# Written-out cross loops, later attention products, and plain expert writes with a read-back, in a three-layer kernel on one core

## The chip, the cores and the metric

The kernel runs on one NeuronCore of a Trainium2 chip. The core has a matmul engine (TensorE, PE in the rows; PEld is its weight load), VectorE (DVE), ScalarE (ACT), GpSimd (POOL), SyncE (SP, which here only starts transfers) and 16 DMA engines. Each engine runs its own stream of instructions; semaphores tie the streams together. The metric is the device time of one execution in microseconds (us). The kernel before takes 898.19 us, the median of three runs between 898.18 and 898.23.

## The reference

x has 32 batches of 32 tokens of width 512 (1024 rows), the context 32 batches of 257 rows. All is fp32.

```
x = x + cross_attention(layernorm(x), ctx)   # 16 heads of 32; q and k are rotated by position;
                                             # softmax over 257 keys; output projection and bias
x = x + self_attention(layernorm(x))         # 16 heads, causal, 32 tokens
n = layernorm(x)
logits = n @ gate_w.T + gate_b               # 8 experts
keep the 2 best experts per row; gate = softmax over these 2
x = x + sum over the 2 of gate[e] * (n @ expert_w[e] + expert_b[e])
```

## The kernel before, in words

**Products.** An fp32 product is made of three products of parts: each operand is split into a high part (rounded by ACT) and a low part (the rest, by DVE or POOL), and `mm3` adds hi x hi, hi x lo and lo x hi over four chunks of 128, 12 matmuls in one PSUM bank. Names that end in `hi` or `lo`, and `wparts`, are such parts.

**Cross stage.** A tile is 128 rows of x, 4 batches; there are 8 tiles, so 32 batches b = 4t + j. `body(t)` writes out the four batches of a tile. Body 0 and body 7 stand in the program as straight code; bodies 1 to 6 are one body in a hardware loop (`Fori`) on each of the five engines, so every engine jumps back five times. For one batch PE does, in this order: the scores of b (64 matmuls on 32x32 pieces of the array, into four banks); K of b+1 (four `mm3`, 48 matmuls); the transposes of the probabilities of b; V of b+1, first half (12 matmuls, lines 723 to 725); one extra product that differs with j (output projection of the tile before, transposes of the normalised rows, q, transposes of q); attention `attend(b)` (64 small matmuls, line 759); `diagonals_spread(b)` (line 767), which spreads the last key's probability and the inverse sum; and V of b+1, second half. On the other engines: ACT evacuates K (`kb`), makes the exponentials (`pr`) and copies the transposed probabilities (`pt`); DVE masks the scores and takes their maximum (`scored`, `nmax`), inverts the sums (`rinv`), makes `kcos`, evacuates V, and in `o_sum` and `o_lo` adds the last key's part, normalises the attention output (`olast`, `osum`, `onorm`) and makes its low part (`otlo`); POOL makes `ksin` and the diagonals (`pdiag`). The scores of b+1 wait for `kcos` and `ksin`. Order on every engine is the order of the code.

**Self attention** is a pipeline over the 8 tiles; the change leaves it as it is. After it DVE computes the routing: a table that gives for each of 23 slots of 128 rows the expert, the row numbers to gather, and the gate of each row. Every row of x appears in two slots, once per chosen expert. Slots that are not full have spare rows.

**Expert stage.** POOL gathers the 128 normalised rows of slot i from the scratch tensor `ffn_xn_scratch` by an indirect DMA (line 1074) into one of four buffers, three slots ahead. PE transposes the rows of slot i+1 (line 1538, 4 matmuls), then multiplies slot i with its expert's matrix (lines 150 to 152, 12 matmuls). ACT and DVE split the transposed rows (lines 1215 and 1518); ACT multiplies the product by the gate into one of two buffers, called `qt` and `kt` (line 1223). POOL then adds it to the rows of `out_dram` by an indirect DMA with an accumulate (line 1087). Since a row may be in two slots, each add first waits for the one before (`s_add`). The small copies and "ticks" on POOL (lines 1064, 1071, 1081) go between the waits and fetch one column of row numbers. Before the first add, SP has stored all of x with the expert biases in it to `out_dram` (lines 1005, 1006); POOL waits for these nine stores.

## Time and profile before

| what | value |
|---|---|
| runs | 898.18, 898.19, 898.23 us |
| the profiled execution: time, span | 897.09 us, 895.3 us |
| mean granted clock of TensorE | 0.944 |
| busy: PE, PE weight load, DVE, ACT, POOL | 792.0, 649.6, 445.3, 346.4, 307.1 us |
| cross stage, self attention and routing, slots, rest | 0 to 585.4, to 766, to 883.2, to 895.3 us |
| DMA queue of SP: data moved | 43.92 MB |
| DMA queue of POOL: data moved | 12.06 MB |

The span is the time from the first to the last instruction of the profiled execution; its time is 1.8 us more. A granted clock of 1.0 is TensorE's full 2.4 GHz, 0.5 is 1.2 GHz. Durations of matmuls overlap, so the distance between two starts tells more than a duration. In a wait, "issue" as releaser means that the engine waited for nothing that the profile shows.

### The profile page before, as it was taken

How to read it: one execution, taken by the hardware profiler on the slowest of the kernel's cores; microseconds unless marked ns; L12 is line 12 of the kernel's file. 1: busy time of each engine (PE TensorE's matmuls, PEld its weight loads, DVE VectorE, ACT ScalarE, POOL GpSimd, SP SyncE). 2: the span in 40 equal slices, each digit the busy share in tenths (PEclk: the TensorE clock that was granted, in tenths of full speed). 3: DMA queues.
4: the chain of work that ended last, by engine and by line, in shares of the span. 5: the costliest groups of instructions: out<-in, count | busy, mean ns of one | idle time of the engine just before them, and what ended most of it. 6: DMA issues, size and time to landing. Idle time of an engine off the chain costs nothing. (4 is left out here: it accounts for less than half of the span.)

```text
span 895.3 us, 22458 instructions
## 1 busy us (share of the span) xinstructions
PE 792.0 (88%) x8896; PEld 649.6 (73%) x8897; DVE 445.3 (50%) x1102; ACT 346.4 (39%) x807; POOL 307.1 (34%) x357
## 2 busy tenths in 40 slices
PE   5999999999999899999989999969999717777764
PEld 5888888888888788788878888847777515555553
DVE  5645645444454564554444555566766589111110
ACT  5434433433433444335334444434454640222221
POOL 1322422332232223223322332232223084477763
PEclk9999999999999999999999999999999755889987
DMA  9430100100010001001000102172000101655553
GB/s 338 169 119 26 49 25 26 44 31 25 27 49 25 27 25 49 27 26 48 27 26 26 30 21 96 48 300 90 22 14 12 37 12 31 165 100 95 103 104 50
DMA packets 18072, 57.33 MB, mean 64 GB/s; under 512 B 2552, under 2 KB 2936, under 8 KB 16064
## 3 DMA queue, kind: packets, MB, share of 16 engines
q1 hardware_dynamic: 12832, 43.92, 13.6%
q0 software_dynamic: 5152, 12.06, 7.6%
q8 instruction: 76, 1.25, 0.6%
q14 instruction: 12, 0.10, 0.0%
HBM read 45.49 MB, written 10.49 MB: 63 GB/s over the span
## 5 line engine op out<-in xcount | busy, mean ns | idle before, releaser
L150 PE MATMUL bank<-chi,wparts 128*128 128x258 f32 x512 | 152.5, 298 | 7.4 <-DVE wparts L606 7.4
L151 PE MATMUL bank<-clo,wparts 128*128 128x258 f32 x512 | 148.1, 289 | 0.0
L152 PE MATMUL bank<-chi,wparts 128*128 128x258 f32 x512 | 148.0, 289 | 0.0
L318 POOL TENSOR_TENSOR pdiag<-pr,const 128x128 f32<-128x128 f32 x32 | 13.0, 408 | 357.4 <-ACT pr L379 357.4
L150 PEld LDWEIGHTS bank<-chi,wparts 128*128 128x128 f32 x512 | 100.4, 196 | 20.8 <-issue 13.4
L312 POOL TENSOR_TENSOR ksin<-kb,const 128x1032 f32<-128x1032 f32 x32 | 98.5, 3078 | 37.0 <-ACT kb L371 37.0
L723 PE MATMUL bank<-wparts,chi 128*128 128x512 f32 x256 | 110.0, 430 | 1.3 <-DVE wparts L589 1.3
L724 PE MATMUL bank<-wparts,chi 128*128 128x512 f32 x256 | 101.1, 395 | 0.0
L151 PEld LDWEIGHTS bank<-clo,wparts 128*128 128x128 f32 x512 | 100.9, 197 | 0.0
L725 PE MATMUL bank<-wparts,clo 128*128 128x512 f32 x256 | 100.8, 394 | 0.0
L152 PEld LDWEIGHTS bank<-chi,wparts 128*128 128x128 f32 x512 | 100.7, 197 | 0.0
L379 ACT ACTIVATE pr<-scored,nmax 128x257 f32<-128x257 f32 x128 | 63.8, 502 | 54.4 <-DVE nmax L549 54.4
L371 ACT ACTIVATE kb<-bank,bias_cols 128x258 f32<-128x258 f32 x128 | 60.5, 473 | 51.1 <-PE bank L152 50.8
L539 DVE TENSOR_TENSOR v<-bank,bias_cross 128x512 f32<-128x512 f32 x64 | 44.1, 689 | 72.5 <-PE bank L725 72.5
L533 DVE TENSOR_TENSOR kcos<-kb,const 128x1032 f32<-128x1032 f32 x32 | 50.4, 1576 | 34.2 <-ACT kb L371 34.2
L392 ACT ACTIVATE othi<-onorm 128x128 fp32r<-128x128 f32 x32 | 9.9, 311 | 136.7 <-DVE onorm L568 136.7
L723 PEld LDWEIGHTS bank<-wparts,chi 128*128 128x128 f32 x256 | 48.6, 190 | 11.2 <-DVE wparts L589 1.7
L725 PEld LDWEIGHTS bank<-wparts,clo 128*128 128x128 f32 x256 | 48.2, 188 | 11.5
L724 PEld LDWEIGHTS bank<-wparts,chi 128*128 128x128 f32 x256 | 48.4, 189 | 9.0
L364 ACT ACTIVATE chi<-craw 128x1032 fp32r<-128x1032 f32 x32 | 34.0, 1064 | 45.9 <-PE bank L725 41.7
L150 PE MATMUL quad<-wparts,othi 128*128 128x512 f32 (+1 forms) x108 | 46.0, 426 | 2.7 <-issue 2.6
L490 DVE TENSOR_TENSOR clo<-craw,chi 128x1032 fp32r<-128x1032 f32 x32 | 45.7, 1430 | 5.2 <-ACT chi L364 5.2
(233 smaller groups left out, 1712.9 us busy)
## 6 DMA issues: line engine op xcount, KB each, us to landing
craw<-ctx_t_dram SPq DMA_DIRECT2D x32, 516.0 KB, 3.3
expert_lo<-weights_dram SPq DMA_DIRECT2D x8, 1024.0 KB, 13.2
wraw<-weights_dram SPq DMA_DIRECT2D x7, 1024.0 KB, 6.1
out_dram<-x SPq DMA_DIRECT2D x9, 256.0 KB, 5.0
x<-x_dram SPq DMA_DIRECT2D x8, 256.0 KB, 7.4
ffn_xn_scratch<-xn SPq DMA_DIRECT2D x8, 256.0 KB, 2.0
wraw<-weights_dram SPq DMA_DIRECT2D x4, 256.0 KB, 5.4
craw<-biases_dram SPq DMA_DIRECT2D x2, 512.0 KB, 4.6
```

The costliest lines, as they stand in the source:

```text
L150: pe.matmul(psum, ahi(c), bhi(c), start=(c == 0), stop=False)
L151: pe.matmul(psum, ahi(c), blo(c), start=False, stop=False)
L152: last = pe.matmul(psum, alo(c), bhi(c), start=False, stop=(c == chunks - 1))
L312: pool.tensor_tensor(ksin[:], kb[:], sink, ALU.mult).then_inc(s_ksin, 1)
L371: act.activation(kb[:, m, :], proj[m % 3][:, 0:LKP], ACT.Identity, bias=bias_cols[:, m:m + 1]).then_inc(s_kev, 1)
L379: act.activation(pr[:, g, 0:LK], sm[g][:], ACT.Exp, bias=nmax[:, g:g + 1], scale=-1.0, accum_out=rsum[:, g:g + 1]).then_inc(s_exp, 1)
L490: dve.tensor_tensor(clo[j % 2][:], craw[j % 2][:], chi[j % 2][:].bitcast(F32), ALU.subtract).then_inc(s_clo, 1)
L533: dve.tensor_tensor(kcos[:], kb[:], cosk, ALU.mult).then_inc(s_kcos, 1)
L539: dve.tensor_tensor(v[j % 2][:, c, :], proj[(4 + c) % 3][:], bias[:, R_BV, :], ALU.add).then_inc(s_vev, 1)
L723: pe.matmul(psum, hi, whi[WV][:, c, :], start=(c == 0), stop=False)
L724: pe.matmul(psum, hi, wlo[WV][:, c, :], start=False, stop=False)
L725: last = pe.matmul(psum, lo, whi[WV][:, c, :], start=False, stop=(c == KC - 1))
```

## The change

It has four parts.

1. The cross stage's hardware loop over tiles 1 to 6 becomes written-out code on all five engines.
2. In the cross stage PE does V's second half right after the first half and the extra product, then `diagonals_spread(b)`, then `attend(b)`, then the scores of b+1. `o_sum(b)`, ACT's `o_hi(b)` and `o_lo(b)` move into batch b+1, behind its masked scores. A signal on PE before the scores and the tick writes on DVE between them go. At the start DVE makes WV's low parts before `kcos`.
3. In the expert stage POOL writes each slot's output with a plain indirect DMA to a scratch tensor `ffn_out_scratch`, in which a row's first and second choice have rows of their own, and spare rows have others. A slot's buffer is one of four (`qt`, `kt`, `q_self`, `k_self`). No write waits for another. The copies and ticks on POOL go, and the slot loops on POOL and ACT are written out; those on PE and DVE stay. The normalised rows are stored one row further down, and row 0 is a filler.
4. The nine early stores of x go. At the end SP waits for all writes, loads both choices of each tile back (16 loads of 256 KB into the space of `expert_lo`), DVE adds them to x (16 additions), and SP stores x (8 stores).

```diff
@@ cross stage (the same on SP, POOL, ACT, DVE, PE)
-                with pe.Fori(1, TILES - 1) as t:
+                for t in range(1, TILES - 1):
                     body(t)
@@ cross stage, PE
-                    pe.sem_inc(s_go, 1)
...
-                        attend(b, j)
-                        diagonals_spread(b)
                         if more:
                             v_product(b + 1, j + 1, 1)
+                        diagonals_spread(b)
+                        attend(b, j)
@@ cross stage, ACT
                         exp(b, 3)
+                        if not (j == 0 and at_start(t)):
+                            o_hi(b - 1, t if j > 0 else t - 1, (j + BT - 1) % BT)
...
-                        o_hi(b, t, j)
@@ cross stage, DVE
-                    dve.memset(tick[:, g:g + 1], 0.0)
...
-                    dve.wait_ge(s_spread, b + 1)
+                    dve.wait_ge(s_av, b + 1)
...
+                w_lo_chunks(WV)
                 k_cos(0)
-                w_lo_chunks(WV)
...
                             masked(b, j, g)
+                        if not (first and j == 0):
+                            o_sum(b - 1)
                         inverse_sums(b)
+                        if not (first and j == 0):
+                            o_lo(b - 1, (j + BT - 1) % BT)
...
-                        o_sum(b)
-                        o_lo(b, j)
@@ expert stage, SP
-                for t in range(TILES):
-                    sp.wait_ge(s_xbias, t + 1)
-                    sp.dma_start(out[t * P:(t + 1) * P, :], x[:, t, :]).then_inc(s_init, 16)
-                sp.dma_start(out[B * S:B * S + P, :], x[:, 0, :]).then_inc(s_init, 16)
+                sp.wait_ge(s_y, SLOTS)
+                for r in range(AHEAD):
+                    sp.wait_ge(s_scatter[r], 16 * len(range(r, SLOTS, AHEAD)))
+                for t in range(TILES):
+                    for k in range(2):
+                        row = 1 + k * B * S + t * P
+                        sp.dma_start(halves[:, 2 * t + k, :], y_d[row:row + P, :]).then_inc(s_half[t // 2], 16)
+                for t in range(TILES):
+                    sp.wait_ge(s_choices, 2 * t + 2)
+                    sp.dma_start(out[t * P:(t + 1) * P, :], x[:, t, :]).then_inc(s_stored, 16)
@@ expert stage, POOL
-                    pool.wait_ge(s_yev, i + 1)
-                    tick(2)
-                    pool.tensor_copy(add_at[r][:], add_row[:, bass.ds(i, 1)]).then_inc(s_acopy, 1)
-                    pool.wait_ge(s_acopy, i + 1)
-                    tick(3)
-                    if not (isinstance(i, int) and i == 0):
-                        pool.wait_ge(s_add, i * 16)
-                        tick(4)
-                    pool.indirect_dma_start(out, bass.IndirectOffsetOnAxis(ap=add_at[r][:], axis=0), ysb[r][:], None,
-                                            compute_op=ALU.add).then_inc(s_add, 16)
+                    pool.wait_ge(s_yev, i + 1)
+                    pool.indirect_dma_start(y_d, bass.IndirectOffsetOnAxis(ap=scatter_row[:, i:i + 1], axis=0),
+                                            ysb[r][:], None).then_inc(s_scatter[r], 16)
@@ expert stage, ACT
-                        act.wait_ge(s_add, (i - 1) * 16)
+                    if i >= AHEAD:
+                        act.wait_ge(s_scatter[r], i // AHEAD * 16)
@@ expert stage, DVE
-                dve.tensor_scalar(gather_row[:], number, 1.0, 1.0, ALU.max, ALU.subtract).then_inc(s_rows, 1)
+                dve.tensor_scalar(second, number, B * S + 0.5, -float(B * S), ALU.is_ge, ALU.mult).then_inc(s_rt, 1)
+                dve.scalar_tensor_tensor(spare, number, 0.0, rc(R_SPARE, SLOTS), ALU.is_equal, ALU.mult).then_inc(s_rt, 1)
+                dve.wait_ge(s_rt, 22)
+                dve.scalar_tensor_tensor(gather_row[:], number, 1.0, second, ALU.max, ALU.add).then_inc(s_rows, 1)
...
+                for t in range(TILES):
+                    dve.wait_ge(s_half[t // 2], 64)
+                    dve.tensor_tensor(x[:, t, :], halves[:, 2 * t, :], x[:, t, :], ALU.add).then_inc(s_choices, 1)
+                    dve.wait_ge(s_choices, 2 * t + 1)
+                    dve.tensor_tensor(x[:, t, :], halves[:, 2 * t + 1, :], x[:, t, :], ALU.add).then_inc(s_choices, 1)
```

On PE, the end of batch 2 before (the extra product, q, stands ahead of these rows; 723 to 725 are V's second half, of whose four rounds the first and the last row are shown, 739 the scores):

```order
L759 MATMUL quad<-pt,v 32x32 x32
L767 MATMUL quad<-pdiag,const 128x256
L723 MATMUL bank<-wparts,chi 128x512
...
L725 MATMUL bank<-wparts,clo 128x512
L739 MATMUL bank<-kcos,qt 32x257
L739 MATMUL quad<-kcos,qt 32x257 x3
```

The same place in the changed kernel, where V is on lines 729 to 731, the spread product on 772, attention on 764 and the scores on 744:

```order
L729 MATMUL bank<-wparts,chi 128x512
...
L731 MATMUL bank<-wparts,clo 128x512
L772 MATMUL quad<-pdiag,const 128x256
L764 MATMUL quad<-pt,v 32x32 x32
L744 MATMUL bank<-kcos,qt 32x257
L744 MATMUL quad<-kcos,qt 32x257 x3
```

V's second half has moved ahead, and the two small products stand directly before the scores, spread first.

On POOL, one slot of the expert stage before, from one add to the next (1087 the add, 1074 the gather, 1071 and 1081 copies of row numbers, 1064 ticks):

```order
L1087 DMA out_dram<-qt,add_at 1152x512
L1064 TENSOR_TENSOR pool_tick<-pool_tick 1x1
L1071 COPY gather_at<-gather_row 128x1
L1064 TENSOR_TENSOR pool_tick<-pool_tick 1x1
L1074 DMA v_self<-ffn_xn_scratch,gather_at 128x512
L1064 TENSOR_TENSOR pool_tick<-pool_tick 1x1
L1081 COPY add_at<-add_row 128x1
L1064 TENSOR_TENSOR pool_tick<-pool_tick 1x1 x2
L1087 DMA out_dram<-kt,add_at 1152x512
```

Two slots and a half of the changed kernel (1083 the write, 1076 the gather):

```order
L1083 DMA ffn_out_scratch<-kt,scatter_row 4993x512
L1076 DMA x3t<-ffn_xn_scratch,gather_row 128x512
L1083 DMA ffn_out_scratch<-q_self,scatter_row 4993x512
L1076 DMA xn<-ffn_xn_scratch,gather_row 128x512
L1083 DMA ffn_out_scratch<-k_self,scatter_row 4993x512
```

Gathers and writes alternate as before, with nothing between them but waits.

## Rows read from the trace of the kernel before

**Rows 1.** Busy time by engine in stretches of the cross stage: straight batches, the loop.

```profile
core 0: us, PE busy (x) PEld busy (x) DVE busy (x) ACT busy (x) POOL busy (x), PEclk, DMA share, GB/s
30.05:99.67 69.62, 69.62 (x898) 59.89 (x897) 34.42 (x100) 30.30 (x81) 24.88 (x14) 0.98 0.18 65
99.67:521.68 422.01, 411.26 (x5257) 349.10 (x5257) 211.67 (x594) 168.76 (x474) 120.49 (x78) 0.98 0.10 32
```

**Rows 2.** Waits of PE: who waited for what, total us, times, longest.

```profile
PE bank L739 <- issue: 10.7, 5, 2.4
```

**Rows 3.** Busy time in the first of four half-clock stretches behind the gaps.

```profile
170.90:174.30 3.40, 3.40 (x17) 3.40 (x17) 1.55 (x12) 1.83 (x6) 0.00 (x0) 0.50 0.00 0
```

**Rows 4.** Timeline at a jump back: start, duration, what, idle before and releaser.

```profile
299.79 3.27 POOL L312 TENSOR_TENSOR ksin<-kb,const 128x1032 f32<-128x1032 f32 x1 [0.36 <-ACT kb L371]
...
307.43 0.39 PE L725 MATMUL bank<-wparts,clo 128*128 128x512 f32 x1
...
310.23 0.37 PE L739 MATMUL bank<-kcos,qt 32*32 32x257 f32 x1 [2.41 <-issue]
```

**Rows 5.** Timeline of PE at the end of batch 25.

```profile
484.63 0.58 PE L723 MATMUL bank<-wparts,chi 128*128 128x512 f32 x1
485.05 0.39 PE L724 MATMUL bank<-wparts,chi 128*128 128x512 f32 x1
...
487.14 0.39 PE L724 MATMUL bank<-wparts,chi 128*128 128x512 f32 x1
487.37 0.39 PE L725 MATMUL bank<-wparts,clo 128*128 128x512 f32 x1
487.69 0.40 PE L739 MATMUL bank<-kcos,qt 32*32 32x257 f32 x1
```

**Rows 6.** Timeline of POOL in the expert stage, one slot.

```profile
799.46 1.61 POOL L1087 DMA_INDIRECT out_dram<-kt,add_at  x1 [0.16 <-issue]
...
801.74 1.03 POOL L1074 DMA_INDIRECT x3t<-ffn_xn_scratch,gather_at  x1 [0.15 <-issue]
...
804.25 0.18 POOL L1064 TENSOR_TENSOR pool_tick<-pool_tick 1x1 f32<-1x1 f32 x1 [0.89 <-DMA out_dram<-kt,add_at]
804.59 1.61 POOL L1087 DMA_INDIRECT out_dram<-qt,add_at  x1 [0.16 <-issue]
```

**Rows 7.** The 23 accumulating writes, line 1087: from issue to landing.

```profile
DMA to landing us min/median/max: 4.5/4.8/6.2
```

**Rows 8.** The 23 gathers, line 1074: from issue to landing.

```profile
DMA to landing us min/median/max: 3.4/4.1/6.2
```

**Rows 9.** Timeline: first matmul of products 0, 1, 2, last of 22, its gating.

```profile
766.08 0.79 PE L150 MATMUL quad<-wparts,xthi 128*128 x1 [0.43 <-issue]
...
770.27 0.47 PE L150 MATMUL quad<-wparts,othi 128*128 x1
...
773.58 0.50 PE L150 MATMUL quad<-wparts,xthi 128*128 x1
...
882.76 0.39 PE L152 MATMUL quad<-wparts,xtlo 128*128 x1
...
883.24 0.69 ACT L1223 ACTIVATE qt<-quad,wraw 128x512 f32<-128x512 f32 x1 [1.98 <-PE quad L152]
```

**Rows 10.** Timeline of the start of the slots.

```profile
757.36 5.96 SPq L1005 DMA_DIRECT2D out_dram<-x  x8
...
761.79 1.09 PE L1538 MATMUL bank<-const,v_self 128*128 128x128 f32 x4 [1.37 <-DMA v_self<-ffn_xn_scratch,gather_at]
...
764.53 1.12 PE L1538 MATMUL bank<-const,x3t 128*128 128x128 f32 x4 [1.66 <-DMA x3t<-ffn_xn_scratch,gather_at]
```

**Rows 11.** Busy time in a load stretch at the kernel's start; last column GB/s.

```profile
11.20:22.40 11.20, 8.78 (x51) 7.69 (x49) 7.75 (x11) 7.45 (x15) 2.45 (x2) 1.00 1.02 392
```

**Rows 12.** Groups by line: DVE's additions to x; after the bar busy us, mean ns.

```profile
L1523 DVE TENSOR_TENSOR x<-bank,x 128x512 f32<-128x512 f32 x4 | 2.5, 684 | 0.0
```

**Rows 13.** DMA issues: stores of the normalised rows, KB each, us to landing.

```profile
ffn_xn_scratch<-xn SPq DMA_DIRECT2D x8, 256.0 KB, 2.0
```

More of the change, by code:

```diff
@@ L345, in _ @@
                 body(0)
-                with pool.Fori(1, TILES - 1) as t:
+                for t in range(1, TILES - 1):
                     body(t)
@@ L472, in body @@
                             qt_evac(t + 1)
-                        o_hi(b, t, j)
                 body(0)
-                with act.Fori(1, TILES - 1) as t:
+                for t in range(1, TILES - 1):
                     body(t)
                 body(TILES - 1, last=True)
+                o_hi(B - 1, TILES - 1, BT - 1)
             @block.vector
@@ L665, in _ @@
                 dve.wait_ge(s_bo, 16)
-                with dve.Fori(1, TILES - 1) as t:
+                for t in range(1, TILES - 1):
                     body(t)
                 body(TILES - 1, last=True)
+                o_sum(B - 1)
+                o_lo(B - 1, BT - 1)
                 dve.tensor_tensor(x[:, TILES - 1, :], x[:, TILES - 1, :], bias[:, R_BO, :], ALU.add).then_inc(s_xb, 1)
@@ L900, in perceiver @@
             gather_row = sb("gather_row", [P, SLOTS], U32)
[L901 to L904 removed]
+            scatter_row = sb("scatter_row", [P, SLOTS], U32)
             used = [R_ALL, 0]
@@ L1060, in _, with gather @@
                     expert_lo_part(e)
-                def tick(cell):
-                    pool.tensor_tensor(pool_tick[:, cell:cell + 1], pool_tick[:, 7:8], pool_tick[:, 7:8], ALU.add)
-                def gather(i, r):
-                    if not (isinstance(i, int) and i < AHEAD):
+                def gather(i):
+                    r = i % AHEAD
+                    if i >= AHEAD:
                         pool.wait_ge(s_ext, i - AHEAD + 1)
-                        tick(0)
-                    pool.tensor_copy(gather_at[r][:], gather_row[:, bass.ds(i, 1)]).then_inc(s_gcopy, 1)
-                    pool.wait_ge(s_gcopy, i + 1)
-                    tick(1)
-                    pool.indirect_dma_start(xg[r][:], None, x3_d, bass.IndirectOffsetOnAxis(ap=gather_at[r][:], axis=0)
+                    pool.indirect_dma_start(xg[r][:], None, x3_d,
+                                            bass.IndirectOffsetOnAxis(ap=gather_row[:, i:i + 1], axis=0)
@@ L1090, in _ @@
                 pool.wait_ge(s_rows, 1)
                 pool.wait_ge(s_x3d, 16 * TILES)
+                pool.wait_ge(s_x3pad, 16)
                 for i in range(AHEAD - 1):
-                    gather(i, i)
+                    gather(i)
                 pool.wait_ge(s_rows, 3)
-                pool.wait_ge(s_init, 16 * (TILES + 1))
-                def expert_step(i, r):
-                    gather(i + AHEAD - 1, (r + AHEAD - 1) % AHEAD)
-                    add(i, r % 2)
-                for i in range(AHEAD):
-                    expert_step(i, i)
@@ L1103, in _ @@
-                with pool.Fori(1, LAST_ROUND) as k:
-                    for r in range(AHEAD):
-                        expert_step(k * AHEAD + r, r)
-                for i in range(LAST_ROUND * AHEAD, SLOTS):
+                for i in range(SLOTS):
                     if i + AHEAD - 1 < SLOTS:
-                        expert_step(i, i % AHEAD)
-                    else:
-                        add(i, i % 2)
+                        gather(i + AHEAD - 1)
+                    scatter(i)
             @block.scalar
@@ L1216, in slot_hi, with gated @@
                                    ACT.Copy).then_inc(s_exhi, 1)
-                def gated(i, r):
+                def gated(i):
+                    r = i % AHEAD
                     act.wait_ge(s_y, i + 1)
-                    if not (isinstance(i, int) and i < 2):
-                        act.wait_ge(s_add, (i - 1) * 16)
-                    act.activation(ysb[r][:], (b_x3, b_cp)[r], ACT.Copy,
-                                   scale=slot_gate[:, bass.ds(i, 1)]).then_inc(s_yev, 1)
+                    if i >= AHEAD:
+                        act.wait_ge(s_scatter[r], i // AHEAD * 16)
+                    act.activation(ysb[r][:], (b_x3, b_cp)[i % 2], ACT.Copy,
+                                   scale=slot_gate[:, i:i + 1]).then_inc(s_yev, 1)
                 slot_hi(0, 0)
                 act.wait_ge(s_rows, 3)
-                def expert_step(i, r):
-                    slot_hi(i + 1, 1 - r)
-                    gated(i, r)
-                for r in range(2):
-                    expert_step(r, r)
-                with act.Fori(1, (SLOTS - 1) // 2) as k:
-                    for r in range(2):
-                        expert_step(k * 2 + r, r)
-                gated(SLOTS - 1, 0)
+                for i in range(SLOTS):
+                    if i + 1 < SLOTS:
+                        slot_hi(i + 1, (i + 1) % 2)
+                    gated(i)
             @block.vector
```

64 lines of the change are left out of this document (31 added, 33 removed).

## The prediction

> **What bounds the kernel now.** I went from the busy time by stage to the waits, then to the timeline where a wait ends, because the change touches two stages that have different limits.
>
> In the cross stage, TensorE (PE) is the limit. The first four batches, written out in the program, keep it busy for 69.62 of 69.62 us; the 24 batches of the loop keep it busy for 411.26 of 422.01 us [rows 1]. The missing 10.75 us are found in the list of waits as one line: before a scores product, five times, released by "issue", 10.7 us, the longest 2.4 us [rows 2]. Six passes of a loop have five jumps back, and the timeline shows one of them: the last V product starts at 307.43, the scores only at 310.23, and nothing they need is late, since ksin, the later operand to be made, was complete at 303.06 [rows 4]. So what is waited for is the instruction stream after the jump. After four of the five gaps a stretch of 3.40 us stands at a granted clock of 0.50 (1.2 instead of 2.4 GHz), with PE fully busy in it (the first of the four: [rows 3]); the engine had been idle for 2 us just before. Half of such a stretch is lost work: 1.7 us each.
>
> In the expert stage no engine is the limit. Per slot, GpSimd (POOL) issues a gather and an accumulating write, and each write first waits until the one before has landed: issued at 799.46, it landed before 804.25, where POOL had been idle for 0.89 us, and the next one follows 5.13 us after the first [rows 6]. A write takes 4.8 us (median) from issue to landing [rows 7]. PE could be faster: product 1 starts at 770.27, product 2 at 773.58, a period of 3.31 us where nothing is awaited; but from product 0 (766.08) to the end of product 22 (882.76 + 0.39 = 883.15) it needs 117.1 us [rows 9], 5.1 us per slot.
>
> **The sum, part by part**, against the profiled execution's own 897.09 us (span 895.3), which lies 1.1 us under the median of 898.19.
>
> (a) *Cross loops written out.* The five gaps go, 10.75 us [rows 1, 2], and with them the four half-clock stretches, 4 x 1.7 = 6.8 us [rows 3]. The straight batches 0 to 3 show what is left: nothing. **-17.5.** Bounds: 0, if the gaps are moved and not removed (a rival below), and -17.5.
>
> (b) *V's second half moved ahead of spread and attention.* PE is the limit here, so only what changes between neighbours on PE counts. Today V's first matmul after the spread product takes 0.42 us to the next (484.63 to 485.05) where the others take 0.23 (487.14 to 487.37), and the step from V's last to the scores takes 0.32 instead of 0.23 [rows 5]. These two extras, 0.19 and 0.09, are 0.28 us a batch; some of them comes back, because V's last now meets the spread product and attention meets the scores. I take 0.1 us for 31 batches: **-3.1**. Bounds: -0.28 x 31 = -8.7, and +3 if two bursts of 64 small matmuls in a row feed worse than with V between them.
> The Trainium skill (TensorEngine Tiling, Key Properties) says that changing the tiling mode drains TensorE. Today a batch changes it four times, afterwards three times. The page has no price; at the 0.19 us of the row above one change less would give 5.9 us for 31 batches instead of 3.1.
>
> What moves with it on the other engines: the sums over spread and attention (three VectorE (DVE) operations and one subtraction) and ScalarE (ACT)'s conversion go into the next batch, behind the masked scores. DVE waits there for the exponentials anyway, before the reciprocal, and the output product reads their result later still. The spread product needs POOL's diagonals, which are made during K and V. ksin is ready at 303.06 and V ends at 307.82 [rows 4], a cover of 4.8 us, of which the move takes 1 us at most. The signal that PE sent before the scores goes too: 0. The four tick writes go from a DVE that is half idle: 0. In the last batch a layer norm now stands ahead of the sums on DVE, with PE's own V product above it: 0. The reordered start (WV's low parts before kcos) moves V forward, but the rotation of q, next on DVE, still comes last: between 0 and 0.9, I take **-0.5**.
>
> (c) *Start of the slots.* A copy and a tick before each gather go, two short DVE operations before the first gather row come; these cancel. The nine stores of x, eight of them in flight from 757.36, leave this place, so that the second gather no longer lands at 764.5 [rows 10]. The first transposes cannot start much before 761.3, since PE waits for the bias sums; then 1.1 us of transposes, conversion and subtraction (0.6 and 0.7) and product 0 at 763.9 instead of 766.08 [rows 9]: **-2.2**. Bounds -1 and -4.
>
> (d) *The slots.* The writes no longer wait for one another, each has a row of its own in a scratch tensor, and there are four output buffers instead of two. What is left is the larger of three periods. PE: 3.31 us. POOL: an indirect write of at most 1.61 us (the accumulating one's time) and a gather of 1.03 us [rows 6], with 0.15 us of issue each, 2.9 us. The chain through a gather buffer: gather i+4 stands behind write i on POOL and is needed by product i+3. From the end of product i: hand-over 0.09, gating 0.69 [rows 9], POOL 0.3, the write 1.61, 0.15, landing of the gather 4.1 (median) [rows 8], 0.2, transposes 0.46, product 2.85: 10.45 us for three slots, 3.48 each; with the shortest landing, 3.4 [rows 8], 3.25. The landings seen are those of gathers that queue behind an accumulating write, and plain writes should hold them up less, so I take 3.37, between the chain's ends and just over PE's own. Product 0 to product 1 stays 4.19 us [rows 9], 21 periods of 3.37 are 70.8, and the last product 2.9: 77.9 instead of 117.1, **-39.2**. Bounds: 3.31 (-40.5), and 4.0 (-26), from a landing of 5.7 us, near the longest seen (6.2 in rows 8).
> By the Trainium skill (DMA: Bandwidth & Descriptors, Anatomy of one DMA) a DMA from GpSimd takes about 2.0 us plus its bytes at 436 GB/s: an estimate of 2.6 us for 256 KB, 3.6 with the 1.03 us of issue, and so a chain of 3.3 us per slot, PE-bound. The rows show 4.1 in the median.
>
> (e) *The new tail.* Today 12.15 us lie between the end of product 22 and the span's end. Afterwards: gating 0.8, the last write 4.8 at most [rows 7], then for the first time a wait for all writes, and 16 loads of 256 KB (4.19 MB). The best stretch of the start moved 392 GB/s at full DMA engines [rows 11]: 10.7 us, plus 2.1 for the way in and out. DVE adds behind the loads; of its 16 additions the last four come after the last landing, 4 x 0.70 = 2.8, by its 0.68 for an addition of this size [rows 12]. The last store is 0.2 and 2.0 us, as for the stores of the normalised rows [rows 13]. The other stores fall between. With 0.3 for the end, 0.8 + 4.8 + 12.8 + 2.8 + 2.2 + 0.3 = 23.7: **+11.6**. Bounds: +8 (a plain write that lands in 3.4, loads that overlap their fixed time) and +22 (loads at half that rate).
>
> Sum: -17.5 - 3.1 - 0.5 - 2.2 - 39.2 + 11.6 = **-50.9**: 846.2 for a profiled execution, with the 1.1 us **847.3** in the median.
>
> **Rivals.**
> *The gather chain binds.* Plain writes go to device memory as the accumulating ones do, and gathers queue behind them; with a gather landing after 5.7 us the period is 4.0. For it: today's landings of up to 6.2 [rows 8], and POOL's 2.9 us close under PE's 3.31. Against: 3.4 is seen also, with an accumulating write in front. -26 instead of -39.2: 861.
> *The read-back is slow.* 2 KB rows, scattered just before, come back at half the rate: 10.7 us more, 858. For it: no row has a read of freshly scattered data. Against: the start's loads are of rows of the same size.
> *The change does not do what it says.* The gaps stay, because it is not the jump that makes them but something that recurs every four batches. For it: "issue" names no cause. Against: the written-out batches 0 to 3 have none [rows 1]. Then (a) is 0: 865.
> *Slower: written-out code starves PE.* Each executed block of instructions now comes from memory once, and if PE waited for it as it does after a jump, 2.15 us plus 1.36 of half clock, once in each of the 24 batches, the cost were 24 x 3.5 = 84 us instead of 17.5, and the result 33 us slower than before, 931. It decides from 2.1 us per batch on. Against: batches 0 to 3 are such code, at 69.62 busy of 69.62 [rows 1].
> By the Trainium skill (Runtime: NRT & Kernel Launch, Instruction fetch mechanics) the sequencer fetches straight code ahead in 16 KiB blocks and only a taken jump out of them stalls; by that rule the starving rival falls away. The rows on batches 0 to 3 agree; none of a straight stretch of 32 batches exists here.
>
> **Chances.** Forecast (840 to 856) 0.66, gather chain 0.14, slow read-back 0.07, gaps stay 0.06, starved PE 0.03, something else of either sign 0.04. The range 838 to 864 leaves out the best ends of all terms together (835) and reaches over the first two rivals. This measurement can tell about 0.2% from no change; faster by more than that: 0.95, within it 0.01, slower 0.04.
>
> **What would show it.** PE: no "issue" wait before the scores, a loop stretch of about 401 us instead of 422 with the clock at 1.00, batches of 15.5 and 17.9 us. Slots: product starts 3.3 to 3.5 us apart, PE idle before transposes near 0; if the chain binds, PE idles before transposes with a gather as releaser in every slot. Tail: about 24 us from the last product to the end, 11 to 13 of them loads at 350 to 400 GB/s. Wrong would be: gaps before the scores in other places, a slot period over 3.7, or a tail over 28.

## The result, and the profile after

The changed kernel takes 848.46 us in the median of four runs (847.62 to 855.45), where the kernel before took 898.21 beside it: a ratio of 0.945, with a 95% interval of 0.939 to 0.951. The forecast was 847.3 us. The profiled execution took 847.62 us, with a span of 845.8 (895.3 before) and a mean granted clock of 0.951. Single runs of one kernel differ by up to 16 us here, and one of the kernel before took 1503.40 us, so the ratios leave out runs more than 1.5% above the shortest of their kernel, and sizes are read from the traces, stage by stage.

The busy time by engine, in the straight batches and in the stretch that was the loop; it answers to [rows 1]:

```profile
core 0: us, PE busy (x) PEld busy (x) DVE busy (x) ACT busy (x) POOL busy (x), PEclk, DMA share, GB/s
31.20:100.73 69.53, 69.53 (x898) 60.04 (x897) 33.97 (x81) 30.61 (x81) 22.05 (x14) 0.98 0.19 67
100.73:501.93 401.20, 401.04 (x5261) 345.01 (x5257) 214.69 (x498) 167.07 (x475) 94.71 (x78) 1.00 0.11 34
```

The 24 batches take 401.20 us instead of 422.01, PE is busy for 401.04 of them, and the clock is 1.00. The list of PE's waits over this stretch is empty; the line of [rows 2] is gone, and so is the stretch of [rows 3].

The timeline of PE at the end of a batch (start, duration, what), as [rows 5]:

```profile
466.84 0.39 PE L731 MATMUL bank<-wparts,clo 128*128 128x512 f32 x1
467.07 0.59 PE L772 MATMUL quad<-pdiag,const 128*128 128x256 f32 x2
467.59 0.76 PE L764 MATMUL quad<-pt,v 128*32 128x32 f32 x64
468.31 0.37 PE L744 MATMUL bank<-kcos,qt 32*32 32x257 f32 x1
```

V's last, the spread, attention and the scores stand there without an idle mark between them.

The timeline of POOL in the expert stage, as [rows 6]:

```profile
763.70 0.99 POOL L1083 DMA_INDIRECT ffn_out_scratch<-qt,scatter_row  x1 [1.24 <-ACT qt L1208]
764.99 0.97 POOL L1076 DMA_INDIRECT v_self<-ffn_xn_scratch,gather_row  x1 [0.30 <-issue]
766.91 0.99 POOL L1083 DMA_INDIRECT ffn_out_scratch<-kt,scatter_row  x1 [0.95 <-ACT kt L1208]
```

A write follows a write after 3.21 us (763.70 to 766.91). POOL now waits for ACT's gated product, which waits for PE. The landing of the writes (line 1083) and of the gathers (line 1076), as [rows 7, 8], and the busy time over 21 periods, from product 1 to product 22:

```profile
DMA to landing us min/median/max: 2.7/2.7/3.2
...
DMA to landing us min/median/max: 3.2/3.4/4.4
```
```profile
749.55:819.96 70.41, 69.71 (x335) 55.67 (x334) 14.52 (x21) 24.52 (x42) 39.23 (x40) 1.00 0.45 149
```

70.41 / 21 = 3.35 us per slot, with PE busy for 69.71 of 70.41. Product 0 starts at 743.98, and product 22 ends at 822.91.

The timeline of the tail, and the busy time in the stretch in which the first loads run:

```profile
823.90 0.97 POOL L1083 DMA_INDIRECT ffn_out_scratch<-q_self,scatter_row  x1 [1.81 <-ACT q_self L1208]
826.78 8.06 SPq L1016 DMA_DIRECT2D expert_lo<-ffn_out_scratch  x16
832.08 0.69 DVE L1513 TENSOR_TENSOR x<-expert_lo,x 128x512 f32<-128x512 f32 x1 [13.51 <-DMA expert_lo<-ffn_out_scratch]
...
842.42 0.69 DVE L1515 TENSOR_TENSOR x<-expert_lo,x 128x512 f32<-128x512 f32 x1
```
```profile
828.00:832.00 4.00, 0.00 (x0) 0.00 (x0) 0.00 (x0) 0.00 (x0) 0.00 (x0) 0.50 0.93 340
```

The last write is issued at 823.90, the loads begin 2.88 us later, the first addition comes 5.3 us after that, and the sixteen additions follow almost without a pause until 843.11. From the last product to the end it is 845.8 - 822.91 = 22.9 us.

### The profile page after: what moved, and what is told of

It reads as the page before. It is cut to its first block and busy times, and to the rows that moved or that the text cites. A ratio compares the mean times of both kernels' runs of the same rounds, so it can differ in the third digit from the quotient of the medians.

```text
span 845.8 us, 21194 instructions
## 1 busy us (share of the span) xinstructions
PE 770.9 (91%) x8896; PEld 642.7 (76%) x8897; DVE 458.9 (54%) x991; ACT 342.1 (40%) x807; POOL 235.7 (28%) x200
## 5 line engine op out<-in xcount | busy, mean ns | idle before, releaser
L152 PE MATMUL bank<-chi,wparts 128*128 128x258 f32 x512 | 150.1, 293 | 8.1 <-DVE wparts L608 8.0
L153 PE MATMUL bank<-clo,wparts 128*128 128x258 f32 x512 | 145.9, 285 | 0.0
L154 PE MATMUL bank<-chi,wparts 128*128 128x258 f32 x512 | 145.8, 285 | 0.0
L152 PEld LDWEIGHTS bank<-chi,wparts 128*128 128x128 f32 x512 | 97.8, 191 | 21.1 <-issue 12.8
L313 POOL TENSOR_TENSOR ksin<-kb,const 128x1032 f32<-128x1032 f32 x32 | 95.3, 2978 | 64.2 <-ACT kb L372 64.2
L729 PE MATMUL bank<-wparts,chi 128*128 128x512 f32 x256 | 105.6, 413 | 0.2 <-DVE wparts L591 0.2
L730 PE MATMUL bank<-wparts,chi 128*128 128x512 f32 x256 | 101.5, 396 | 0.0
L154 PEld LDWEIGHTS bank<-chi,wparts 128*128 128x128 f32 x512 | 98.4, 192 | 0.0
L153 PEld LDWEIGHTS bank<-clo,wparts 128*128 128x128 f32 x512 | 98.3, 192 | 0.0
L536 DVE TENSOR_TENSOR kcos<-kb,const 128x1032 f32<-128x1032 f32 x32 | 39.4, 1230 | 33.4 <-ACT kb L372 33.4
L731 PEld LDWEIGHTS bank<-wparts,clo 128*128 128x128 f32 x256 | 48.5, 189 | 11.6
L551 DVE CUSTOM_DVE_ANT_0 scored<-bank,mb 128x257 f32<-128x257 f32 x32 | 13.7, 427 | 54.9 <-PE quad L744 54.9
```

What stands on the lines that cost most here:

```text
L152: pe.matmul(psum, ahi(c), bhi(c), start=(c == 0), stop=False)
L153: pe.matmul(psum, ahi(c), blo(c), start=False, stop=False)
L154: last = pe.matmul(psum, alo(c), bhi(c), start=False, stop=(c == chunks - 1))
L313: pool.tensor_tensor(ksin[:], kb[:], sink, ALU.mult).then_inc(s_ksin, 1)
L536: dve.tensor_tensor(kcos[:], kb[:], cosk, ALU.mult).then_inc(s_kcos, 1)
L729: pe.matmul(psum, hi, whi[WV][:, c, :], start=(c == 0), stop=False)
```

## The experiments

Each kernel but the first is the changed one with the edit that is shown. They ran in three groups, each with the kernel before beside it: the one with the cross stage alone, the one in which the other engines loop and the two with PE's loop (893.68 us for the kernel before, in the median), the one with the old order and the three with other writes (896.75), and the last four (896.25). Each ratio is to the kernel before of its own group, and it says only in which direction the time went.

**Which part of the gain is whose.** The cross stage as changed, all else as before:

```
cross stage of the changed kernel; expert stage and tail of the kernel before
```

> The kernel before with the cross stage of the changed one, the expert stage as before. Theory (the two halves of the change add up): the cross stage is worth 21.4 us by the starts of the first and last scores in the two traces, the expert stage with its tail 28: 876 to 879. Rival (the stages depend on each other, by the clock or by the transfers of the expert weights): outside 874 to 881.

Measured: 878.36 us, ratio 0.9855 (0.9771 to 0.9939). The trace is clearer than the times. The busy time by engine (columns as above) from the scores of batch 31 to the end of the span:

```profile
547.63:872.40 324.77, 241.54 (x2010) 180.66 (x2002) 151.63 (x306) 110.63 (x171) 145.08 (x248) 0.87 0.32 81
```

Before, the same stretch (570.35 to 895.3) takes 324.95 us. So of the difference of the spans, 22.9 us, all but 0.2 lies ahead of batch 31, and the two halves of the change don't touch each other.

**The order alone, in written-out code:**

```diff
                         if more:
-                            v_product(b + 1, j + 1, 1)
-                        diagonals_spread(b)
                         attend(b, j)
+                        diagonals_spread(b)
+                        v_product(b + 1, j + 1, 1)
```

DVE's sums wait for the spread product again, which now comes after attention.

> The changed kernel, but on PE V's second half stands behind attention and spread again, as before the change; the later sums on DVE and ACT stay, and so does the dropping of ticks and signal. Theory (the 0.17 us by which a batch became shorter come from PE's order alone: 0.42 instead of 0.23 behind the spread product, 0.32 instead of 0.23 before the scores): 31 x 0.17 = 5.3 us more, 852 to 854. Rival (they come from the signal and the ticks that were dropped): as the changed kernel, 847 to 849.

Measured: 857.17 us, ratio 0.9539 (0.9462 to 0.9615). The busy time from the scores of batch 1 to those of batch 31, in this kernel, in the changed one and in the kernel before:

```profile
59.21:562.39 503.18, 503.18 (x6558) 427.14 (x6557) 269.72 (x617) 211.15 (x593) 118.60 (x97) 1.00 0.12 39
```
```profile
51.33:550.08 498.75, 498.59 (x6560) 428.83 (x6556) 268.98 (x617) 210.14 (x593) 118.65 (x97) 1.00 0.12 39
```
```profile
50.13:570.35 520.22, 509.48 (x6558) 432.55 (x6557) 265.57 (x736) 213.56 (x593) 149.36 (x97) 0.99 0.12 38
```

Writing out, in the old order, is worth 520.22 - 503.18 = 17.0 us. This kernel differs from the one before also in the dropped signal and ticks and in the later sums, but the 17.0 us leave nothing for these: 10.7 of them are time in which PE was idle (520.22 - 509.48), and 6.3 are busy time (509.48 - 503.18), close to the 6.8 that the half-clock stretches were taken to cost. The order, in written-out code, is worth 503.18 - 498.75 = 4.4 us in 30 batches, 0.15 each, where the expectation had 0.17; since signal and ticks are missing in both kernels, its rival is out. The rest of what this kernel lost (its first batch, 29.0 us instead of 20.1) has another cause, told below.

**One engine at a time.** All engines but PE loop (with DVE's tick writes back, which a loop on DVE needs here):

```diff
-                for t in range(1, TILES - 1):
+                with sp.Fori(1, TILES - 1) as t:      # the same on POOL, ACT, DVE
                     body(t)
```

> The mirror of it: PE written out, SP, POOL, ACT and DVE with the hardware loop (and DVE's tick writes, which its loop form needs). Theory (PE pays for its own jumps alone; the others' jumps fall into their idle time, since each of them is under 55% busy): 847 to 850, no gap before the scores. Rival (their jumps reach PE through a late mask, kcos or ksin): gaps with ACT, DVE or POOL as releasers, 850 to 864.

Measured: 853.07 us, ratio 0.9559 (0.948 to 0.9638), span 845.8, and 498.92 us from batch 1 to batch 31. The loops of the other engines cost 498.92 - 498.75 = 0.2 us: only PE's matters. Now PE alone loops (with its signal before the scores back):

```diff
-                for t in range(1, TILES - 1):
+                with pe.Fori(1, TILES - 1) as t:
                     body(t)
```

> The changed kernel, but with tiles 1 to 6 of the cross stage in a hardware loop on PE alone (with the signal before the scores, which the loop form needs); the four other engines stay written out. Theory (PE's own jump back costs it 2.15 us of idle and in four of five cases 1.7 us of half clock): five gaps before the scores, about 16.7 us more than the changed kernel's 847.6, so 863 to 866. Rival 1 (the gap is made by the jumps of the engines that feed PE): no gap, 847 to 849. Rival 2 (something that recurs every four batches, whatever the program form): no gap either, since the changed kernel has none, 848.

Measured: 887.12 us, ratio 0.9933 (0.989 to 0.9976). The expectation missed by over 20 us. The stretch from batch 1 to batch 31 takes 536.8 us instead of 498.8, and the first batch 28.9 instead of 20.1, which is told below. With half as many jumps:

```diff
-                for t in range(1, TILES - 1):
-                    body(t)
+                with pe.Fori(1, (TILES - 2) // 2 + 1) as k:
+                    body(k * 2 - 1)
+                    body(k * 2)
```

> As the kernel with PE's loop, but a pass holds two tiles, so that the loop jumps back twice instead of five times. Theory (a fixed price per jump, whatever the length of the pass): two gaps of about 2.15 us, 4.3 to 7.7 us over the changed kernel with the half clock, so 852 to 856. Rival (the price grows with the code that a pass holds, since more has to come from memory): two gaps of about 4 us each, 858 or more.

Measured: 864.58 us, ratio 0.9685 (0.9594 to 0.9776): above the upper end of the expectation and on its rival's side. The list of PE's waits, over batches 4 to 27, of the kernel with five jumps and of the one with two:

```profile
PE bank L746 <- issue: 27.2, 6, 5.6
```
```profile
PE bank L746 <- issue: 12.2, 7, 5.3
```

Before it was 10.7 us for five [rows 2]. Five of the first kernel's idle times are 5.1 to 5.6 us, two of the second's 5.2 and 5.3; the others are under 0.5. So the gaps go with PE's jumps, and a jump's idle time has become two and a half times as long. Either the new order uncovered it, or the other engines' written-out code competes for the fetch. So all five engines loop again (with signal and ticks), with the new order in the body:

```diff
-                for t in range(1, TILES - 1):
+                with pe.Fori(1, TILES - 1) as t:      # and on SP, POOL, ACT, DVE
                     body(t)
```

> All five engines go round the cross loop as in the kernel before, with the new order of the products in its body; gathers, writes and tail are those of the changed kernel. In the runs so far a jump back cost 1.9 to 2.4 us in the kernel before (all loop, V's second half last) and 5.1 to 5.6 us where TensorE alone loops with the new order. Theory O, the order uncovers the jump: V's second half, 48 long products standing ahead of the jump, let TensorE's sequencer reach the jump some 2.6 us before the array ran dry; behind the new order stands the attention product, which waits for VectorE, so nothing covers the fetch. Then all five gaps are 5.0 to 5.7 us here too, and the time is that of the PE loop without its slow first batch: about 880 to 886 us. Theory C, the written-out code of the other four engines competes for the fetch: then the gaps are 1.9 to 2.4 us and the time is about 864 to 868 us. A slow first batch (29 instead of 20 us) may add 9 us to either.

Measured: 886.96 us, ratio 0.9887 (0.9845 to 0.993), on the side of theory O. (V's second half is 12 matmuls, not the 48 of the expectation.) The wait line and the stretch from batch 1 to batch 31:

```profile
PE bank L747 <- issue: 27.6, 7, 5.7
```
```profile
52.28:589.21 536.93, 509.29 (x6560) 436.20 (x6557) 271.45 (x737) 208.85 (x593) 118.85 (x97) 0.97 0.11 37
```

The gaps at the five jumps are 5.2 to 5.7 us with all engines looping; competition is out, and the order is what uncovers the jump. The timeline at the first jump of this kernel, and at that of the kernel before (the last rows of PE ahead of the jump, and the scores behind it):

```profile
167.40 0.59 PE L775 MATMUL quad<-pdiag,const 128*128 128x256 f32 x2
...
167.92 0.76 PE L767 MATMUL quad<-pt,v 128*32 128x32 f32 x64
173.97 0.60 PE L747 MATMUL bank<-kcos,qt 32*32 32x257 f32 x1 [5.29 <-issue]
```
```profile
164.14 0.58 PE L723 MATMUL bank<-wparts,chi 128*128 128x512 f32 x1
...
166.88 0.39 PE L725 MATMUL bank<-wparts,clo 128*128 128x512 f32 x1
169.28 0.37 PE L739 MATMUL bank<-kcos,qt 32*32 32x257 f32 x1 [2.01 <-issue]
```

And the instruction queue around the two jumps, from the view of the DMA traffic (one digit or number for each 0.2 us from 168, then each 0.25 us from 160):

```profile
GB/s 0 0 0 0 0 82 0 82 0 0 0 0 0 0 0 0 0 0 0 0 0 0 0 0 0 0 0 0 0 0 82 0 0 0 0 0 0 0 0 0
...
q8 instruction: 3, 0.05, 3.9%
```
```profile
GB/s 149 215 347 429 429 248 50 0 0 0 0 0 0 0 0 0 0 0 66 0 66 0 0 0 0 0 0 0 0 0 0 0 0 0 0 0 0 66 0 0
...
q8 instruction: 3, 0.05, 2.8%
```

Each jump fetches two blocks of 16 KB (82 GB/s for 0.2 us, 66 for 0.25). With the new order they start at 169.1 and 169.6, after the last attention row has ended (168.68), and the scores start 4.9 us after the first. In the kernel before they start at 164.7 and 165.1, while PE has only begun V's second half (164.14 to 167.27), and the scores start 4.6 us after. The pair belongs to PE's jump: where PE alone loops it stands at 176.5 and 176.8, with the scores at 181.36, and where the four others loop and PE does not, no two blocks of this queue start closer than 3.4 us in the cross stage. The latency is nearly the same; before, 2.6 us of it lay under V's twelve products (164.7 to 167.27), and with the new order nothing lies over it. Why the fetch starts so early behind V's products and only after attention is not shown: attention has waits in front of it, which may hold back PE's sequencer, and its 64 products are also over in 0.8 us.

So the two edits of the cross stage are not a sum (us from batch 1 to batch 31; the written-out kernels are without signal and ticks, which by the 17.0 us above cost nothing):

| | V's second half last | attention last |
|---|---|---|
| loop | 520.2 (before) | 536.9 |
| written out | 503.2 | 498.8 (changed) |

The new order gains 4.4 us in written-out code and loses 16.7 in the loop.

**The writes.** Plain writes, each waiting for the one before; accumulating writes that don't wait; and both. The two accumulating kernels also fill the scratch tensor by 20 transfers beside the cross stage, so their sums hold these numbers too:

```diff
                     pool.wait_ge(s_yev, i + 1)
+                    if i > 0:
+                        pool.wait_ge(s_scatter[(i - 1) % AHEAD], 16 * ((i - 1) // AHEAD + 1))
                     pool.indirect_dma_start(y_d, ...
-                                            ysb[r][:], None)
+                                            ysb[r][:], None, compute_op=ALU.add)
```

> The changed kernel, but each plain write waits until the one before has landed, as the accumulating writes did. The changed kernel's trace has plain writes of 0.99 us on POOL that land 2.7 us after issue. Theory A (the gain of the slots comes from the cheaper write, not from its independence): write to write at least 2.7 + 0.3 = 3.0 us, under PE's 3.35 per slot: no change, 847 to 850. Rival B (independence made the gain): the period goes to 4 us or more, 862 or more.

> The changed kernel, but the writes accumulate into their rows of the scratch tensor, each row once, without waiting for one another; so that the scratch has finite numbers it is filled by 20 transfers beside the cross stage, and the sums then hold these numbers too. Theory A (the accumulating write itself is dear, 1.61 us on POOL and 4.8 to land, and holds up the gather queued behind it): the chain over a gather buffer gives 3.4 to 3.6 per slot instead of 3.35, 2 to 6 us more, 850 to 855. Rival B (only the waits between the writes cost): as the changed kernel, 847 to 849.

> Both together: accumulating writes that wait for one another, as before the change, but without the copies and ticks on POOL and with four buffers. Theory (the round trip of one accumulating write sets the slot): 4.8 + 0.3 = 5.1 us per slot, 22 x 1.75 = 38 us more, 884 to 889. Rival (the copies and ticks on POOL set it before): under 870.

Measured: serial 856.36 us, ratio 0.9564 (0.9486 to 0.9643); accumulating 872.24 us, 0.9745 (0.9672 to 0.9818); both 901.74 us, 1.0061 (1.002 to 1.0103). The busy time over the same 21 periods, in that order:

```profile
745.92:819.71 73.79, 71.00 (x336) 55.54 (x334) 14.52 (x21) 24.57 (x42) 39.23 (x40) 1.00 0.43 142
```
```profile
747.84:832.24 84.40, 73.14 (x336) 56.03 (x334) 14.52 (x21) 25.39 (x42) 52.13 (x40) 0.98 0.70 123
```
```profile
750.87:864.12 113.25, 83.89 (x335) 60.21 (x334) 14.53 (x21) 26.15 (x42) 50.59 (x39) 0.92 0.52 90
```

| us per slot | independent | serial |
|---|---|---|
| plain | 3.35 (changed) | 3.51 |
| accumulating | 4.02 | 5.39 |

A plain write of 2.7 us fits into a period of 3.35 nearly even when it must have landed: the expectation of no change missed by 0.16 us per slot, 3.4 in all. (The median of 856.36 lies above the 847 to 850 that it gave; of that the slots explain 3.4 us.) So the waits for one another were costly only because the writes accumulated. An accumulating write occupies POOL for 1.59 instead of 0.99 us, keeps the DMA engines busy for 0.70 instead of 0.45 of the time for the same 10.4 MB, and delays the gather behind it: PE waits for gathers here (7 times, 7.1 us), and in the changed kernel only its weight load does, once, for 0.3 us. That is the gather chain of the first rival, at the 4.0 us that it gave, though PE waits in a third of the slots and not in every one; the landing of these gathers isn't in the trace. My expectation of 850 to 855 for the independent accumulating writes, and the one of 884 to 889 for both, missed it. In the last one the period of 5.39 lies 0.16 over that of the kernel before, which took 109.92 us for the same 21 periods (770.27 to 880.19), 5.23 each. So the copies and ticks on POOL had not set it; where the 0.16 us come from stays open. The tail is 33.2 us, since the last write is issued only at 875.98, 8.9 us after the last product.

**The tail.** The changed kernel again; one semaphore for each tile's two loads; and beside that four of the additions on POOL:

```diff
-                        sp.dma_start(halves[:, 2 * t + k, :], y_d[row:row + P, :]).then_inc(s_half[t // 2], 16)
+                        sp.dma_start(halves[:, 2 * t + k, :], y_d[row:row + P, :]).then_inc(s_half[t], 16)
...
-                    dve.wait_ge(s_half[t // 2], 64)
+                    dve.wait_ge(s_half[t], 32)
...
+                for n, t in enumerate((1, 4)):        # the last kernel only: these two tiles on POOL
+                    pool.wait_ge(s_half[t], 32)
+                    pool.tensor_tensor(x[:, t, :], halves[:, 2 * t, :], x[:, t, :], ALU.add).then_inc(s_padded, 1)
...
```

> The changed kernel once more, as the level for the other three of this call and for its own scatter (847.6 to 855.5 us in its first four runs). Theory P: the scatter is the first batch, where VectorE's short operations now and then start under one of GpSimd's long ones and end only with it, so that TensorE waits for the last parts of the context: spans of about 846 us with a first batch of 20 us and about 854 us with one of 29 us. Rival: the scatter lies in the granted clock of the stages behind the cross stage; then the first batch is 20 us in a slow profile too. Median 847 to 856 us.

> A semaphore for each tile's two loads at the end in place of one for each four. If the tail is the first megabyte and then sixteen adds of 0.665 us back to back, the first add starts two loads (0.5 MB at about 370 GB/s, 1.4 us) sooner and everything behind it with it: tail (end of the last product to the end of the span) 21.5 instead of 22.9 us, time 1.4 us below the changed kernel's. If the loads bind the tail, as the prediction had it, no change: 22.9 us.

> As the one with a semaphore for each tile, and GpSimd takes the four adds of two tiles off VectorE's sixteen. If the two engines add side by side, the adds take 12 x 0.665 = 8.0 us in place of 11.0 (GpSimd's four, at about 1.1 us by its 4.5 us for four times the elements, lie beside them): tail 21.5 - 2.8 = about 18.7 to 19.5 us, with the loads then close to binding. If an add of three SBUF operands on VectorE and one on GpSimd exclude each other, as the stretched first batch suggests, the adds take 8.0 + 4 x 1.1 = 12.5 us and the tail is 22.5 to 23.5 us, no better than the changed kernel's 22.9.

Measured: again 849.15 us (847.8 to 855.38), ratio 0.9472 (0.9429 to 0.9515); a semaphore for each tile 853.32 us (845.7 to 858.37), 0.9512 (0.9458 to 0.9567); shared 852.63 us (847.5 to 860.83), 0.948 (0.9426 to 0.9534). None is clear of the changed kernel: the intervals overlap. With the finer semaphores the first addition starts 3.3 instead of 5.3 us after the loads, and the last ends 1.0 us earlier against their start (15.3 instead of 16.3 us, and 16.9 in the changed kernel's second profile), but the end doesn't move: 846.0 - 822.74 = 23.3 us. The busy time of this kernel in its tail:

```profile
832.00:836.00 4.00, 0.00 (x0) 0.00 (x0) 3.90 (x7) 0.00 (x0) 0.00 (x0) 0.50 1.01 379
836.00:840.00 4.00, 0.00 (x0) 0.00 (x0) 3.81 (x7) 0.00 (x0) 0.00 (x0) 0.50 1.03 371
840.00:843.00 3.00, 0.00 (x0) 0.00 (x0) 1.63 (x3) 0.00 (x0) 0.00 (x0) 0.50 1.05 405
843.00:846.00 3.00, 0.00 (x0) 0.00 (x0) 0.00 (x0) 0.00 (x0) 0.00 (x0) 0.50 0.55 210
```

The DMA engines are full until 843, while DVE has become idle (its last addition ends at 841.92): 16 loads and 8 stores, 6.29 MB, at about 375 GB/s are 16.8 us, and these are most of the tail. My theory that the additions bind it has fallen. Additions (15.3 us) and transfers are about equally long, so shortening one alone should gain little; that both together would gain is not tested.

In the shared kernel the tail is 853.5 - 830.04 = 23.5 us, at the upper end of what the expectation gave for engines that exclude each other (22.5 to 23.5). The transfers would hold it there anyway, so only the rows tell, where an addition of POOL and one of DVE overlap:

```profile
844.16 1.26 POOL L1102 TENSOR_TENSOR x<-expert_lo,x 128x512 f32<-128x512 f32 x1 [1.84 <-DMA expert_lo<-ffn_out_scratch]
844.24 1.74 DVE L1524 TENSOR_TENSOR x<-expert_lo,x 128x512 f32<-128x512 f32 x1
845.50 1.62 POOL L1104 TENSOR_TENSOR x<-expert_lo,x 128x512 f32<-128x512 f32 x1
845.90 1.78 DVE L1522 TENSOR_TENSOR x<-expert_lo,x 128x512 f32<-128x512 f32 x1
```

DVE's addition takes 1.74 us instead of 0.69: it ends 0.6 us after POOL's, as if it had started there, and POOL's next takes 1.62 instead of 1.26. The two take turns.

## Why the prediction was right

Term by term, from the two profiled executions and the experiments:

| term | predicted | measured | read from |
|---|---|---|---|
| (a) cross loops written out | -17.5 | -17.0 | before against the old order written out (batches 1 to 31) |
| (b) V's second half ahead | -3.1 | -4.4 | the same kernel against the changed one |
| start in another order | -0.5 | not told from scatter | scores of batch 0 at 30.05 before, 29.1 to 31.2 in the others |
| (c) start of the slots | -2.2 | -1.8 | scores of batch 31 to product 0: 195.73 and 193.90 |
| (d) slots | -39.2 | -38.1 | 117.07 and 78.93 |
| (e) tail | +11.6 | +10.7 | 12.15 and 22.9 |

With 1.2 us of the start (first scores 30.05 before, 31.20 after) they make the -49.5 of the spans, up to rounding.

(a) was right in its cause too: the idle time belonged to the jump and went with it, and the half-clock stretches behind it. In the kernel whose PE loop has five jumps, a half-clock stretch of 3.4 to 6.8 us begins in or just behind every gap. The starved-PE rival is out: 32 straight batches have no issue wait, as batches 0 to 3 said. The rival that the gaps stay is out as well: there is none in the written-out code, and two where PE jumps twice.

(b) was the least founded term, 0.1 us a batch between bounds of -0.28 and +0.1; it is 0.15. What I did not see is that its sign hangs on (a). I costed the two edits one by one and added them; the rows to see it stood in my own groups: in [rows 4] the wait of 2.4 us follows on V's products, and I did not ask when the fetch began. The sum held because the change does both. By the rule on drained modes that the prediction set beside this term (Trainium skill, TensorEngine Tiling, Key Properties), at the price that it took from a row, it would have been 5.9 us; the 4.4 us lie between the two, and no run here separates the mode changes from the rest of the order.

(c) came as forecast: PE waits for DVE's bias sums until 741.36, and the second transposes follow without a wait.

(d): the period was 3.37 forecast and 3.35 measured. The forecast was a middle between the chain's two ends (3.25 and 3.48), and what binds is PE, busy for 69.71 of 70.41 us, so that it came within 0.02 is partly luck. The first rival didn't come because the chain through the gather was shorter than feared: a plain write costs POOL 0.99 us, not 1.61, and the gather lands in 3.4, not 4.1. The prediction's estimate from the Trainium skill (DMA: Bandwidth & Descriptors, Anatomy of one DMA) for that gather, 3.6 us with its issue, was nearer to the measured 3.4 than the 4.1 of the rows. Product 0 to product 1 took 5.6 instead of 4.2 us, at half clock; this is the 1 us by which (d) fell short.

(e): the sum was right and its split was not. I had the write at 4.8 (it is 2.7), the loads at 12.8 and four additions of 0.7 behind them. In truth the stores share the rate with the loads, and 6.29 MB bind, not 4.19. The loads begin 3.9 us after the last product instead of 5.6, and from there to the end it takes 19.0 us instead of 18.1; that the two errors nearly cancel is luck. The rival of a slow read-back is out: the loads alone ran at 340 GB/s from 828 to 832, with the DMA engines busy for 0.93 of the time.

## What to carry to other kernels

Before you cost a loop that is written out and an order that is changed in its body as two terms, look where in the timeline the instruction fetch of the jump begins: it is covered by what the engine has queued, and the value of either edit depends on the other. Here twelve long products at the end of the body covered 2.2 to 2.8 us of each jump, and 64 short ones with waits in front covered nothing. An indirect write that accumulates is dearer than a plain one in its issue, in its landing and in what queues behind it; with places of their own for all rows, 23 writes gave back 38 us, and the read-back took 11 of them. Where a stage streams at the full rate of the DMA engines, count loads and stores together.

## What the runs showed of the hardware

**DVE and POOL take turns.** The first batch takes 20.1 us in the changed kernel's profile and 21.8 in its second; in nine others it takes 18.9 to 22.2 us, but 29.0 in the kernel with the old order, 28.9 with the PE loop and 29.4 with the shared tail. The timeline of the kernel with the old order shows why:

```profile
39.34 2.21 POOL L313 TENSOR_TENSOR ksin<-kb,const 128x1032 f32<-128x1032 f32 x1
39.41 2.43 DVE L501 TENSOR_SCALAR xn<-x,mv,rstd 128x512 f32<-128x512 f32 x1 [0.67 <-POOL rstd L172]
41.52 4.67 POOL L332 TENSOR_TENSOR wparts<-wraw,wparts 128x2048 fp32r<-128x2048 f32 x1
41.76 4.58 DVE L644 TENSOR_TENSOR last_parts<-last_raw,last_parts 128x128 fp32r<-128x128 f32 x1
```

DVE's two operations take 2.43 and 4.58 us, since each starts just after a long one of POOL and ends 0.1 to 0.3 us after it. The first takes 0.55 us where it starts 0.2 us ahead of POOL's, as in the changed kernel (39.09 against 39.26). The second takes 0.28 us where nothing is in its way, and it is the one that decides. That operation and POOL's in the kernel with the cross stage alone, where the batch takes 18.9 us:

```profile
40.87 0.28 DVE L641 TENSOR_TENSOR last_parts<-last_raw,last_parts 128x128 fp32r<-128x128 f32 x1
41.16 5.54 POOL L330 TENSOR_TENSOR wparts<-wraw,wparts 128x2048 fp32r<-128x2048 f32 x1 [0.50 <-ACT wparts L355]
```

In nine of the fourteen profiles `xn` is stretched to 2.4 us or more; six of these have a batch of 18.9 to 22.2 us, and the three long ones are those in which `last_parts` starts 0.1 to 0.3 us behind POOL's `wparts`. A race of some 0.2 us decides over 7 us and more: in the kernel with the old order PE waits 5.1 us for the parts, and the granted clock from 48 to 58 us is 0.53, where it is 0.93 in the changed kernel. (In the kernel with serial writes and in the one where all engines loop, `kcos` is hit instead, at 5.6 us instead of 1.2, and the batch takes 19.0 and 22.2 us. In the changed kernel's own profile `last_parts` takes 1.36 us, behind `ksin`.) By the Trainium skill (SBUF — State Buffer, Terms) the two engines share a pair of ports that one holds for its whole instruction while the other is blocked; the trace agrees. It fits the single runs of 855 us among those of 848, in both series of the changed kernel, and in the kernel with the PE loop the profiled run with the long batch (894.05 us) is one of three at 893.7 to 894.7, seven others being at 884.5 to 887.5. No profile of such a run of the changed kernel exists, so that this is their cause is argued and not shown.

**A jump** of PE costs nearly the same latency whether one engine loops or all five, 4.6 to 5.1 us from the first fetch to the scores in all seventeen jumps of four kernels; PE's idle time is what is left of it behind the products that still run: 1.9 to 2.4 us behind V's, 5.1 to 5.7 behind attention.
